# An LSTM recurrence of 1250 steps: the order of two pairs of hidden units in the step is rearranged on three engines

## The reference

```python
def step(carry, x_t):
    h_prev, c_prev = carry
    combined = jnp.concatenate((x_t, h_prev), axis=1)      # 512 + 512
    f_t = sigmoid(combined @ W_f + b_f)
    i_t = sigmoid(combined @ W_i + b_i)
    c_tilde = tanh(combined @ W_c + b_c)
    c_t = f_t * c_prev + i_t * c_tilde
    o_t = sigmoid(combined @ W_o + b_o)
    h_t = o_t * tanh(c_t)
    return (h_t, c_t), h_t
_, hs = jax.lax.scan(step, (h0, c0), x_over_the_1250_nodes)
```

## Time and profile before

| | us |
|---|---|
| median of 3 executions | 6511.76 (6509.95 to 6512.96) |
| the profiled execution | 6517.52 |
| its span in the trace | 6515.7 |
| recurrence in it, first matmul of L1658 to L2026 | 1262.8 to 5553.7 |

### The profile page before, as it was taken

The page is one execution under the profiler, slowest core; times in us unless marked ns, Lnnn a source line. Parts: engine busy times, 40 slices in busy tenths (PEclk is TensorE's granted clock), DMA queues, the critical chain, the costliest instruction groups (busy, mean ns, idle before and its releaser), DMA issues. The chain is left out here.

```text
span 6515.7 us, 407469 instructions
## 1 busy us (share of the span) xinstructions
PE 5245.6 (81%) x179041; PEld 3598.1 (55%) x179041; DVE 3797.7 (58%) x22378; ACT 1840.6 (28%) x8915; POOL 680.9 (10%) x716
## 2 busy tenths in 40 slices
PE   1968958789777898778987778987777777887999
PEld 1433424667555666556665556765555555554545
DVE  7328867566666666666666666666666666574111
ACT  1201058333333333333333333333333333200000
POOL 0545446000000000000000000000000000251000
PEclk8989978899999999999999999999999999997999
DMA  2235456101000000000000000000000000221110
GB/s 90 79 67 148 129 148 195 53 26 29 0 0 0 17 28 16 0 0 7 27 27 0 0 0 24 29 6 0 0 0 0 0 0 0 83 79 52 68 39 10
DMA packets 173533, 240.46 MB, mean 37 GB/s; under 512 B 90537, under 2 KB 131113, under 8 KB 169794
## 3 DMA queue, kind: packets, MB, share of 16 engines
q0 software_dynamic: 41952, 116.33, 6.5%
q1 hardware_dynamic: 131298, 120.73, 6.1%
HBM read 224.38 MB, written 12.61 MB: 36 GB/s over the span
## 5 line engine op out<-in xcount | busy, mean ns | idle before, releaser
L1658 PE MATMUL l_bank<-l_w,l_hp 128*32 128x128 f16 x160000 | 2471.0, 219 | 797.7 <-DVE l_hp L1961 786.6
L1658 PEld LDWEIGHTS l_bank<-l_w,l_hp 128*32 128x32 f16 x160000 | 2247.3, 97 | 1397.7 <-DVE l_hp L1961 1382.3
L1925 DVE STREAM_TRANSPOSE agg<-l_bank 128x128 f32<-128x128 f32 x2500 | 793.5, 317 | 1135.6 <-PE l_bank L1658 960.2
L1801 ACT ACTIVATE l_th<-l_z 128x8 f32<-128x8 f32 x2500 | 523.2, 209 | 2112.5 <-DVE l_z L1931 2112.5
L1668 PE MATMUL l_spare<-l_w 128*2 128x512 f16 x12056 | 859.6, 379 | 10.1 <-issue 2.5
L2147 POOL DMA_INDIRECT ga_rows<-r_table,dst_t x176 | 167.6, 952 | 4601.7 <-DMA r_table<-c_r 4473.1
L1806 ACT ACTIVATE l_tc<-l_th 128x2 f32<-128x2 f32 x2500 | 490.7, 196 | 466.0 <-DVE l_th L1948 466.0
L1937 DVE SCALAR_TENSOR_TENSOR l_terms<-l_th 128x4 f32<-128x4 f32 x2500 | 357.7, 143 | 255.9 <-ACT l_th L1801 255.9
L1955 DVE TENSOR_TENSOR l_hp<-l_go,l_tc 128x2 f16<-128x2 f32 x2500 | 422.1, 169 | 132.8 <-ACT l_tc L1806 2.3
L1931 DVE TENSOR_REDUCE l_z<-agg 128x8 f32<-128x24 f32 x2500 | 446.7, 179 | 42.6
L1961 DVE TENSOR_TENSOR l_hp<-l_full,l_hp 128x2 f16<-128x2 f32 x2500 | 422.5, 169 | 44.5 <-DVE l_full L1956 0.8
(11 more groups left out here) (425 smaller groups left out, 4856.2 us busy)
## 6 DMA issues: line engine op xcount, KB each, us to landing
w<-in_g_W SPq DMA_DIRECT2D x128, 128.0 KB
w<-in_l_Wx SPq DMA_DIRECT2D x128, 128.0 KB
keys<-in_src_by_tile SPq DMA_DIRECT2D x7, 1344.0 KB, 6.3
e_w<-in_e_W SPq DMA_DIRECT2D x2, 4096.0 KB
e_chosen<-chosen SPq DMA_DIRECT2D x24, 256.0 KB, 5.9
wh<-in_l_Wh SPq DMA_DIRECT2D x1, 4096.0 KB, 18.8
late<-in_l_Wh SPq DMA_DIRECT2D x8, 512.0 KB
late<-in_l_Wx SPq DMA_DIRECT2D x1, 4096.0 KB
```

What stands on the lines that cost most here:

```text
L1658: mm = pe.matmul(banks[par][q][32 * j:32 * j + 32, 0:128], hp[:, par, k, 30 - 30 * v:62 - 30 * v], w16[:, half, k, j, 256 * q + 128 * v:25 ...
L1801: act.activation(th[:, 2 * q:2 * q + 2, 1:], z[:, q, :].rearrange("p (j m) -> p j m", m=GATES), ACT.Tanh, scale=2.0 ** -Z_BITS).then_inc(s ...
L1925: dve.transpose(turn[:, par, q, :, 1:33], banks[par][q][:, 0:128].rearrange("p (m r) -> p m r", r=32)).then_inc(s_turned[q], 1)
```

## The change

In PE's step one group of 4 matmuls of `rows(par, 1, 1)` is issued ahead of the wait for s_h[1], its other three stay behind. In ACT's step the first pair's cell tanh comes ahead of the second pair's gate tanh. In DVE's step `cell_sum` of the first pair comes ahead of `add_up` of the second, `high` of the first pair ahead of `cell_terms` of the second, and `low` of the first pair ahead of `cell_sum` of the second. The number of instructions and their operands stay the same.

```diff
+PARTS = ((0, 0), (0, 1), (1, 0), (1, 1))
...
-            def rows(par, q, k, first=False, signal=None):
-                for half in range(2):
-                    for v in range(2):
-                        for j in range(4):
...
+            def rows(par, q, k, first=False, signal=None, groups=PARTS):
+                for half, v in groups:
+                    for j in range(4):
...
                 rows(par, 1, 0, first=True)
+                rows(par, 1, 1, groups=PARTS[0:1])
                 pe.wait_ge(s_h[1], t + 1)
                 rows(par, 0, 2)
                 rows(par, 0, 3, signal=s_gates[0])
-                rows(par, 1, 1)
+                rows(par, 1, 1, groups=PARTS[1:])
                 rows(par, 1, 2)
                 rows(par, 1, 3, signal=s_gates[1])
...
                                    scale=2.0 ** -Z_BITS).then_inc(s_tanh[q], 1)
-                for q in range(2):
                     act.wait_ge(s_cell[q], t + 1)
...
                 open_gate(t, 0)
+                cell_sum(t, 0)
                 add_up(t, par, 1)
-                cell_sum(t, 0)
+                high(t, par, 0)
                 cell_terms(t, 1)
-                high(t, par, 0)
+                low(t, par, 0)
                 cell_sum(t, 1)
-                low(t, par, 0)
                 open_gate(t, 1)
                 high(t, par, 1)
                 low(t, par, 1)
```

More of the change, by code:

```diff
@@ L1652, in first_rows @@
                                 norm_step(0, i)
-            def rows(par, q, k, first=False, signal=None):
-                for half in range(2):
-                    for v in range(2):
-                        for j in range(4):
[L1658 to L1662, removed]
+            def rows(par, q, k, first=False, signal=None, groups=PARTS):
+                for half, v in groups:
+                    for j in range(4):
+                        mm = pe.matmul(banks[par][q][32 * j:32 * j + 32, 0:128],
+                                       hp[:, par, k, 30 - 30 * v:62 - 30 * v],
+                                       w16[:, half, k, j, 256 * q + 128 * v:256 * q + 128 * v + 128],
+                                       start=first and half == 0 and v == 0,
+                                       stop=k == KC - 1 and half == 1 and v == 1)
                 if signal is not None:
```

## The result

The changed kernel takes 6482.42 us (median of 5 runs, 6479.84 to 6485.84) against 6511.25 us for the kernel before beside it: ratio 0.9959, 95% interval 0.9948 to 0.9970. That is 29 us less. The forecast was 50 us less, 6462, with a range of 6430 to 6508; the time lies in the range and on the side that was given 0.83, and the gain is a little over half of the one forecast.

What follows compares the result with a forecast made beforehand. The first pair's loop, 3.41 us a step, bounds the kernel; afterwards the second pair's, 3.37, would: 0.04 x 1250 = 50 us less, 6467.5 from the profiled 6517.5, median 6462; range 6430 to 6508.

Steps and rivals of the forecast that it cites:

- What bounds the kernel: Recurrence step: one loop of 2.02 us PE and 1.39 us first-pair small instructions; the second pair has 0.07 of room.
- The small instructions: DVE and ACT in each step: first pair reaches PE 0.08 us earlier, at 1.31; second pair 0.09 later, at 2.08.
- rival 2: On DVE, `high` starts 0.06 us after its tanh, not 0.03; 31 us more, 6543; chance 0.10.
- the first way of rival 3: On DVE, only one of the two `high` loses the 0.03; period 3.40, some 6506 us; chance 0.07 for both ways.
- the reason that the prediction gave: Second pair's `high` on DVE started 0.06 after its tanh's end, not 0.03, because `open_gate` ended only at 3.52.
- the second way of rival 3: DVE starts `add_up` only when `cell_sum` is done, 0.54 not 0.47; period 3.40, 6506 us; chance 0.07 for both ways.
- rival 1: The second pair reaches PE in time, by 2.04; period 3.33, 100 us less, 6412; chance 0.08.
- the missing idle time inside the row: Sign in PE's matmul row: about 0.04 us idle was expected; its absence would mean the second pair came in time.
- the second pair's loop: From second transpose over the second pair's arrival at PE to the next: 2.08 + 1.29 = 3.37 us, setting the period.
- the restart: PE from the second pair's arrival to the next second transpose: 1.35 us for 80 matmuls, 1.29 with 76 left.
- the disturbed steps: The odd steps outside the usual pattern in the recurrence: 25 us lost in all, left as it is.
- The cover of the first pair's gates: First gate tanh ends before `cell_terms` starts on DVE: of 0.11 us cover, 0.05 is left after the group's 0.06 delay.

Runs made afterwards that it cites:

- e2: The kernel before with only the group of four matmuls moved ahead of the wait, DVE and ACT in the old order; 6462.68 us, ratio 0.9999.
- e7: The changed kernel with the six DVE calls back in the old order, ACT left as changed; 6642.27 us, ratio 1.0277.
- e1: The changed kernel with its matmul group put back behind the wait, only the DVE and ACT order new; 6500.74 us, ratio 1.0058.
- e3: The changed kernel with two groups, 8 matmuls, ahead of the wait in place of one; 6433.81 us, ratio 0.9953.
- e4: The changed kernel with three groups, 12 matmuls, ahead of the wait in place of one; 6500.82 us, ratio 1.0060.
- e5: The changed kernel with one more group issued between the two calls that end the first pair's gate sums; 6488.88 us, ratio 1.0039.
- e6: The changed kernel with the old order on ACT, both gate tanhs ahead of both cell tanhs; 6655.66 us, ratio 1.0297.

## Why the prediction was right, and where it was off

**What bounds the kernel** held. The loop over the first pair, 2.02 of PE and 1.39 of small instructions, makes up the whole period of 3.41, and the second pair had some room: in e2 four more matmuls ahead of its wait gain nothing.

**The small instructions** came out within 0.02 each. `cell_sum` 0.40 (0.39), `add_up` 0.48 (0.47), cell tanh 0.60 (0.58), gate tanh 0.71 (0.70), `high` 0.83 (0.81), second `cell_terms` 0.98 (0.97), first `low` 1.10 (1.09), PE 1.32 (1.31), second `low` 1.87 (1.86); forecast in brackets. Both `high` started 0.03 after their tanh's end (5007.07 + 0.20, 5007.30; 5007.84 + 0.20, 5008.07), so rival 2 and the first way of rival 3 are out. The 0.06 of the kernel before fits the reason that the prediction gave: in the medians it is there again in e2 and e7, where `open_gate` ends 0.04 ahead of the second pair's tanh, and it is 0.03 in every version where `open_gate` ends 0.17 or more ahead. `add_up` started 0.08 behind `cell_sum`, which takes 0.16, so the second way of rival 3 is out too.

**PE** waits in mid-row, against rival 1, and its row is 0.05 longer for it (0.04 forecast). By the prediction's own list the missing idle time inside the row would have spoken for rival 1; that sign was badly chosen, since earlier matmuls hide the wait. What rules rival 1 out is the period (3.39, not 3.33), the pause in the weight loads, and e1, where four more matmuls behind the wait cost their full 0.055.

**The term that was mis-sized** is the second pair's loop, 2.08 + 1.29 = 3.37, which measured 2.09 + 1.30 = 3.39. The first 0.01 is there from the first pair's `cell_sum` on (0.40 for 0.39), and stays through the second pair's `cell_terms`, `cell_sum` and `low`; it cannot be put down to one instruction when each spacing is read to 0.01. (`cell_sum` itself starts from its wait now and takes 0.164 in the median, against 0.157 in the second pair's row from which its spacing of 0.19 was taken; it measured 0.197.) The second 0.01 is the reading of the restart to two digits: in e1 the same 80 matmuls take 1.355, not 1.35. Both are small beside a step, but the gain is a difference of loops of 3.4 us: 0.02 of the expected 0.04 went with them, 0.02 x 1250 = 25 of 50 us. The other half of the forecast and a few us more in the disturbed steps, which the prediction left as they were, make the 29 measured. I had allowed for just this (6437 to 6487), and the time lies in it.

**The cover of the first pair's gates** was wrong, though it did not touch the number. The prediction let it shrink from 0.11 to 0.05. It compared starts (tanh ready, `cell_terms` started), and e3, e4 and e5 show that an instruction starting from its wait ends 0.05 later than one starting behind the transpose. Compared by ends, an estimate from these rows, a `cell_terms` that started from its wait in the kernel before would end at 0.10 + 0.03 + 0.16 = 0.29 (0.30 from the medians), where the real one ends at 0.36: the cover was 0.06, just the 0.056 that the group takes, and about 0.01 is left. The third loop, which the prediction did not have, is only 0.01 shorter than the second. That the sum held although this loop is missing in it is luck: by the 0.01 that e5 leaves, one more matmul (0.014) ahead of the end of the first pair's gate sums would already have made it the longest.

**What stays open**: why a DVE instruction ends later when it starts from a wait at the same moment was seen and not explained. No version tried beats the changed kernel. The second pair's loop and the crossing loop, both at 3.39, share the way from `cell_terms` to the second pair's `low`; whether fewer or shorter instructions there would gain anything was not tried.

## What to carry to other kernels

When two streams share engines in a hand-written order, write down each loop (where it leaves an engine, where it comes back) and its length; moving one stream ahead gains only down to the next loop, and independent work belongs ahead of the wait that the slower one then exposes, but no more of it than the wait needs: it delays the other stream's results (e3, e4). Compare ends, not starts, when you judge how much cover a step has. Orders on two engines that feed each other must be changed together (e6, e7).

## What the runs showed of the hardware

- The same DVE instruction on 128x4 elements took 0.12 us right behind a transpose and 0.16 to 0.17 when it started from a semaphore wait, with starts only 0.01 apart; the instruction that depends on it came 0.05 later (e3 and e5 against the changed kernel).
- A wait in the middle of a row of matmuls showed no idle time of PE here, since earlier matmuls were still in flight: nothing in the timeline, 0.05 in the length of the row, and a pause in the weight loads.
- PE's weight loads reach the wait sooner than 0.014 a matmul suggests: in the kernel before the 53rd starts 0.68 behind the first, where 52 x 0.014 is 0.73. A late restart is partly won back. Loads that came 0.03, 0.09 and 0.15 late (e3, the changed kernel, e1; medians) made the row 0, 0.05 and 0.10 longer, some 0.04 less each time.
